# Recurrent attention and windowed attention in one kernel: the order of work between the two attentions, the places of VectorE's normalisations, and the banks at the head of a sequence

## The reference, cut to what matters

```
xn = layernorm(x)
# layer 0: gated recurrent attention, 16 heads of 16, times a mixture of 8 experts (top 2)
q, k, v = xn@Wq, xn@Wk, xn@Wv;  gate = exp(log_sigmoid(xn@Wgk1@Wgk2 + bgk2) / 16)
state = state * gate + outer(v, k);  out = state . q            # scan over the tokens
s = (layernorm(out) * gamma + beta) * silu(xn@Wg) @ Wout
f = sum over the top 2 experts e of gates[e] * (relu(xn@Wd[e] + bd[e]) @ Wu[e] + bu[e]) / 2
x = x + s * silu(f)
xn = layernorm(x)
# layer 1: attention in a window of 64 keys, 16 heads on 2 key heads, times a feed-forward net
s = softmax(q . k_window) . v_window @ Wo + bo
f = ternary(w_proj) applied to relu(ternary(w_fc) xn + gate * low-rank term)^2
x = x + s * silu(f)
```

## Time and profile before

| | |
|---|---|
| Time, median of 3 runs | 3416.82 us (3414.13 to 3417.32) |
| Profiled execution, its own time | 3419.85 us |
| Span of that execution (first to last instruction) | 3418.1 us |
| PE busy | 3286.0 us, 96% of the span |
| DVE, ACT, POOL busy | 2671.5 us (78%), 1834.8 us (54%), 1272.6 us (37%) |
| Chain that ended last, by engine | PE 71%, DVE 12%, ACT 7%, DMA 4%, issue 3%, POOL 1% |
| Granted TensorE clock, mean | 0.997 |

### The profile page before, as it was taken

The page is one execution under the profiler, slowest core; times in us unless marked ns, Lnnn a source line. Parts: engine busy times, 40 slices in busy tenths (PEclk is TensorE's granted clock), DMA queues, the critical chain, the costliest instruction groups (busy, mean ns, idle before and its releaser), DMA issues.

```text
span 3418.1 us, 89893 instructions
## 1 busy us (share of the span) xinstructions
PE 3286.0 (96%) x35134; PEld 2274.5 (67%) x35134; DVE 2671.5 (78%) x6395; ACT 1834.8 (54%) x4088; POOL 1272.6 (37%) x1404
## 2 busy tenths in 40 slices
PE   5999999999999999999999999999999999999998
PEld 3676666766667666676766667666676666766666
DVE  6877878878788777887778777787877878878787
ACT  3364654646546465463655636456364654646546
POOL 4434244242443524425233342423434244242432
PEclk9999999999999999999999999999999999999999
DMA  4002010020100202011020110202002010020110
GB/s 116 22 22 61 23 53 19 25 58 24 52 23 25 54 24 61 15 38 40 24 64 11 54 29 21 63 12 65 18 24 60 24 52 21 22 58 24 52 23 26
DMA packets 110005, 128.56 MB, mean 38 GB/s; under 512 B 23457, under 2 KB 77329, under 8 KB 109585
## 3 DMA queue, kind: packets, MB, share of 16 engines
q1 hardware_dynamic: 104720, 121.13, 13.7%
q10 hardware_dynamic: 4864, 1.69, 0.2%
HBM read 74.01 MB, written 17.30 MB: 27 GB/s over the span
## 4 chain that ended last, share of the span: by engine, by line
PE 71%; DVE 12%; ACT 7%; DMA 4%; issue 3%; POOL 1%; SPq 0%; DVEq 0%; ACTq 0%; POOLq 0%
PE bank L1926 7%; PE bank L1549 5%; PE bank L1945 5%; PE bank L1828 5%; PE bank L1694 4%; PE bank L1863 4%; PE bank L1889 4%; PE bank L1586 3%; DMA g_wide<-gate_rows 3%; PE bank L1711 3%; PE bank L1766 3%; PE bank L1666 3%; PE bank L1651 3%; DVE am L1268 3%; PE bank L1845 2%
## 5 line engine op out<-in xcount | busy, mean ns | idle before, releaser
L901 POOL TENSOR_TENSOR qx<-qx 128x512 f32<-128x512 f32 x256 | 277.5, 1084 | 656.9 <-ACT qx L1139 655.1
L1403 DVE TENSOR_REDUCE row_max<-bank 128x4 f32<-128x384 f32 x512 | 270.8, 550 | 90.6 <-PE bank L1828 90.1
L1268 DVE TENSOR_TENSOR am<-bank,causal 128x512 f32<-128x512 f32 x512 | 327.9, 682 | 17.6 <-PE bank L1666 17.6
L1509 DVE TENSOR_TENSOR sq_lo<-qx,sq_hi 128x512 fp32r<-128x512 f32 x256 | 232.3, 907 | 125.3 <-ACT sq_hi L1127 124.1
L1945 PE MATMUL bank<-pj_t,sq_hi 128*128 128x256 f32 x1024 | 260.3, 288 | 6.2 <-DVE sq_lo L1509 5.5
L1023 ACT ACTIVATE tanh_g<-bank 128x256 f32<-128x256 f32 x128 | 49.2, 384 | 400.8 <-PE bank L1549 400.8
L1549 PE MATMUL bank<-w_vg,xt 128*128 128x512 f32 x512 | 252.3, 615 | 0.0
L1945 PE MATMUL bank<-pj_t,sq_lo 128*128 128x256 f32 x1024 | 251.0, 279 | 0.0
L1586 PE MATMUL bank<-xt,w_down 128*128 128x512 f32 x512 | 237.2, 596 | 0.0
L1139 ACT ACTIVATE qx<-bank,scale_fc 128x512 f32<-128x512 f32 x256 | 177.2, 692 | 98.5 <-PE bank L1931 96.6
L1412 DVE TENSOR_TENSOR am<-bank,row_max 128x384 f32<-128x384 f32 x384 | 212.9, 554 | 9.8
(11 more groups left out here) (278 smaller groups left out, 8523.1 us busy)
## 6 DMA issues: line engine op xcount, KB each, us to landing
g_wide<-gate_rows SPq DMA_DIRECT2D x64, 512.0 KB, 6.1
x<-in_L_attn_x SPq DMA_DIRECT2D x128, 128.0 KB, 2.3
qt<-in_L_attn_x SPq DMA_DIRECT2D x128, 128.0 KB, 2.5
out<-x SPq DMA_DIRECT2D x128, 128.0 KB, 1.7
k<-k SPq DMA_DIRECT2D x96, 128.0 KB, 2.4
xl<-xh SPq DMA_DIRECT2D x48, 128.0 KB, 2.4
xl<-xn SPq DMA_DIRECT2D x48, 128.0 KB, 2.3
xh<-xn SPq DMA_DIRECT2D x48, 128.0 KB, 2.3
```

The lines of the kernel that those rows point to most:

```text
L901: nc.gpsimd.tensor_tensor(sq[:, n % 3, :], relu[:, n % 3, :], relu[:, n % 3, :], ALU.mult)\
L1268: nc.vector.tensor_tensor(am_tiles[:, :, j], bank[3 + j][:].rearrange("p (f e t) -> p f e t", f=2, e=2), causal[:].unsqueeze(1).unsqueeze( ...
L1403: nc.vector.tensor_reduce(row_max[:, j, :], bank[1 + j][:, 0:4 * KW].rearrange("p (h k) -> p h k", k=KW), AX.X, ALU.max, negate=(j == 0)). ...
L1509: nc.vector.tensor_tensor(sq_lo[:, n % 3, :], sq[:, n % 3, :], sq_hi[:, n % 3, :].bitcast(F32), ALU.subtract)\
```

## The change

It has three parts. (1) At the head of a sequence `experts_down(0)` to `(3)` and `first_queries_keys(6)` write to other banks, with other waits; ScalarE evicts the gate rows ahead of the queries 4 and 5. (2) On VectorE `finish_chunk(4)` moves from the end of chunk 5 into chunk 6, and two of the four `normalise2` of chunk 6 move behind `project_gated(5)`. (3) On PE `queries(0)` moves ahead of `output_project(7)`, to bank 2 instead of 5; `chunk_turn(7)` moves from behind `score_quad(0)` to the middle of `window_values(0)`.

```diff
+    down_banks = (2, 3, 7, 6)
+    first_banks = {2: 6, 3: 7, 4: 4, 5: 5, 6: 2, 7: 7}
-    qk_banks = (5, 1, 6, 0)
+    qk_banks = (2, 1, 6, 0)
 # ScalarE: first_queries_keys reads bank[first_banks[n]] instead of bank[4 + n % 4],
 # experts_relu reads bank[5 if g else down_banks[j]] instead of bank[5 if g else j]
                     experts_relu(0)
                     experts_relu(1)
-                    first_queries_keys(4)
-                    first_queries_keys(5)
                     for b in range(NG):
                         act.wait_ge(s["gtp_ok"], at("gtp_ok", b + 1))
                         nc.scalar.copy(gate_rows[:, b * 512:(b + 1) * 512], bank[gate_banks[b]][32:64, :]).then_inc(s["gx_ok"], 1)
+                    first_queries_keys(4)
+                    first_queries_keys(5)
                     experts_relu(2)
 # VectorE, chunk c
-                        if 2 <= c < NC - 2:
+                        if 2 <= c < NC - 1:
                             finish_chunk(c - 2)
                         if c == NC - 2:
                             dve.wait_ge(s["rs2"], at("rs2", 1))
-                            for b in range(4):
+                            for b in range(2):
                                 normalise2(b)
...
                             if c:
                                 project_gated(c - 1)
-                            if c == NC - 3:
-                                finish_chunk(c - 1)
+                            if c == NC - 2:
+                                for b in range(2, 4):
+                                    normalise2(b)
                             middle_state(c + 1)
 # PE, first_queries_keys
                         elif n >= 6:
-                            pe.wait_ge(s["qk_ok"], at("qk_ok", n - 5))
+                            pe.wait_ge(s["hr_ok"], at("hr_ok", 1 if n == 6 else 3))
 # PE, experts_down
-                        if i == 0:
-                            pass
-                            if copy:
-                                pe.wait_ge(s["lg_ok"], at("lg_ok"))
-                        elif i == 1:
-                            pass
-                            if copy:
-                                pe.wait_ge(s["hqk_ok"], at("hqk_ok"))
+                        if i in (2, 3):
+                            pe.wait_ge(s["qk_ok"], at("qk_ok", 4 - i))
 # PE, before the turns of the gates
                     pe.wait_ge(s["gates_ok"], at("gates_ok", 7))
-                    pe.wait_ge(s["hr_ok"], at("hr_ok", 2))
+                    if copy:
+                        pe.wait_ge(s["lg_ok"], at("lg_ok"))
 # PE, cumulate(0)
                             pe.wait_ge(s["qk_ok"], at("qk_ok", 3))
-                            pe.wait_ge(s["hr_ok"], at("hr_ok", 4))
+                            pe.wait_ge(s["hr_ok"], at("hr_ok", 2))
 # PE, parity_scores(0)
                             pe.wait_ge(s["qk_ok"], at("qk_ok", 5))
+                            pe.wait_ge(s["hr_ok"], at("hr_ok", 4))
 # PE, queries
-                        if n == 0:
-                            pe.wait_ge(s["f1_ok"], at("f1_ok", NC))
-                        elif n == 1:
+                        if n == 1:
                             pe.wait_ge(s["f2_ok"], at("f2_ok", NC - 1))
 # PE, window_values
                         for w in range(NC):
+                            if part == 0 and w == NC // 2:
+                                pe.wait_ge(s["sg_ok"], at("sg_ok", NC))
+                                chunk_turn(NC - 1)
 # PE, between the attentions
                     pair_turn(2)
                     queries(1)
                     output_turn(NC - 1)
+                    queries(0)
                     output_project(NC - 1)
-                    queries(0)
                     chunk_turn(6)
                     pe.wait_ge(s["low_ok"], at("low_ok", 1))
-                    pe.wait_ge(s["qk2_ok"], at("qk2_ok", 1))
+                    pe.wait_ge(s["qk2_ok"], at("qk2_ok", 2))
                     score_masks(0)
-                    pe.wait_ge(s["qk2_ok"], at("qk2_ok", 2))
                     score_quad(0)
-                    pe.wait_ge(s["sg_ok"], at("sg_ok", NC))
-                    chunk_turn(NC - 1)
                     window_values(0)
```

More of the change, by code:

```diff
@@ L917, in first_queries_keys @@
                         act.wait_ge(s["qkp_ok"], at("qkp_ok", n - 1))
-                        nc.scalar.copy((kt if which else qt)[:, half, g * 512:(g + 1) * 512], bank[4 + n % 4][:])\
+                        nc.scalar.copy((kt if which else qt)[:, half, g * 512:(g + 1) * 512], bank[first_banks[n]][:])\
                           .then_inc(s["qk_ok"], 1)
@@ L940, in experts_relu @@
                             act.wait_ge(s["gkl_ok"], at("gkl_ok", NC // 2))
-                        nc.scalar.activation(hidden_t[g][:, j, :], bank[5 if g else j][:], ACT.Relu, bias=b_down[:, j:j + 1])\
+                        nc.scalar.activation(hidden_t[g][:, j, :], bank[5 if g else down_banks[j]][:], ACT.Relu, bias=b_down[:, j:j + 1])\
                           .then_inc(s["hr_ok"], 1)
@@ L1566, in first_queries_keys @@
                         elif n >= 6:
-                            pe.wait_ge(s["qk_ok"], at("qk_ok", n - 5))
+                            pe.wait_ge(s["hr_ok"], at("hr_ok", 1 if n == 6 else 3))
                         w = w_k if which else w_q
                         for k in range(KD):
-                            mm = nc.tensor.matmul(bank[4 + n % 4][:], w[:, k, half * P:(half + 1) * P],
+                            mm = nc.tensor.matmul(bank[first_banks[n]][:], w[:, k, half * P:(half + 1) * P],
                                                   xt[:, k, g * 512:(g + 1) * 512], start=(k == 0), stop=(k == KD - 1))
@@ L1576, in experts_down @@
                         g, j = i // 4, i % 4
-                        if i == 0:
-                            pass
-                            if copy:
-                                pe.wait_ge(s["lg_ok"], at("lg_ok"))
-                        elif i == 1:
-                            pass
-                            if copy:
-                                pe.wait_ge(s["hqk_ok"], at("hqk_ok"))
+                        if i in (2, 3):
+                            pe.wait_ge(s["qk_ok"], at("qk_ok", 4 - i))
                         for k in range(KD):
-                            mm = nc.tensor.matmul(bank[5 if g else j][:], w_down[:, k, j * P:(j + 1) * P],
+                            mm = nc.tensor.matmul(bank[5 if g else down_banks[j]][:], w_down[:, k, j * P:(j + 1) * P],
                                                   xt[:, k, g * 512:(g + 1) * 512], start=(k == 0), stop=(k == KD - 1))
```

## The result

The changed kernel takes 3448.79 us (median of 4 runs, 3440.83 to 3453.05) against 3417.07 for the kernel before: ratio 1.0091, 95% interval 1.0074 to 1.0108, some +31 us. I had forecast 3425.4 us with a range to 3433, so the direction was right and the size was not.

A forecast was written before the change was run, and what follows sets the result against it. The prediction took TensorE (PE), busy 96% of the span, to bound the kernel, so only its waits counted. Terms -2.6 + 8.0 + 3.2 = +8.6 us on the median 3416.82 gave 3425.4 us, range 3411 to 3433.

The forecast's parts named there:

- the rest comes back as a longer wait at L1694: Sequence head, experts_up(0): PE's saved 1.38 us is kept only as far as GpSimd's product comes earlier; wait near 2.2 us.
- the -2.6 us that I took: Part 1's term: gate rows land 0.15 us earlier in 15 sequences and 0.4 in the first.
- the -0.4 that the rule cited from the Trainium skill's page gave: Part 1 if a DMA's semaphore write lands only after that engine's earlier writes: earlier issue behind the loads brings nothing.
- the gain at the issue: Sequence head: SP's write of the gate rows goes out 0.45 us earlier, right behind the loads of x.
- the lower of my two bounds: Part 1, sequence head: a gain of 0 us a sequence; the other bound was 0.45.
- the pull-in of 0.83 us: Chunk 6 on VectorE: its L1760 comes 5.64 us after its scores instead of 6.47.
- the sum into x at 1.17 us: Chunk 6 on VectorE: the moved sum runs beside GpSimd's product and was forecast to take 1.18 us.
- PE's wait before the second pair: Chunk 6: PE waits for normalised rows before pair_turn(1), so token_major(7) starts 0.5 us later, +8.0 us in all.
- The delay of queries(2): Between the attentions: output_project(7) ends 1.1 us later, so queries(2) starts 0.2 us later a sequence, +3.2 us in all.
- the product of GpSimd: Rival, sequence head: product in time, PE keeps its whole lead of 20.7 us; 3407.3 us, chance 0.08.
- the last turn of x: Rival, between the attentions: this turn is in time and part 3 gains 0.74 us a sequence; 3410.4 us, chance 0.07.
- a full gain at the head: Rival: gate rows land the full 0.45 us earlier, part 1 is -6.0, total 3422.0 us; 0.27 together with an unslowed sum into x.

The follow-up runs named there:

- e1: Part 1 alone on the kernel before: 3433.92 us, ratio 1.0038.
- e2: Part 1 on the kernel before, plus 16 extra identity turns per sequence ahead of experts_up(0) to keep PE busy in its wait: 3419.16 us, ratio 0.9998.
- e9: Part 1 on the kernel before, with the dropped wait for hr_ok 2 put back ahead of the gates' turns: 3416.14 us, ratio 0.9999.
- e6: Kernel before with only finish_chunk(4) moved into chunk 6, all four normalisations left in place: 3424.87 us, ratio 1.0017.
- e13: Part 3 on the kernel before, plus seven extra identity turns in PE's wait ahead of the last turn of x: 3420.64 us, ratio 1.0012.
- e8: Part 1 on the kernel before, with SP's eight loads of x issued behind the first broadcast of the gate rows: 3398.95 us, ratio 0.9940.
- e4: Part 3 alone on the kernel before: 3425.49 us, ratio 1.0025.
- e10: Kernel before with only SP's eight loads of x moved behind the first broadcast of the gate rows: 3409.92 us, ratio 0.9983.

## Why the prediction was right or wrong

**Part 1 (-2.6 us forecast, +16 measured): the step that failed.** It is the sentence "the rest comes back as a longer wait at L1694 (1.02 + 1.38 us less the gain)". The wait is as long as that (2.34 us on average), but I priced it at its own length, as if the matmuls behind it were the same. There was no term for the clock, neither in the sum nor among the bounds nor among the rivals. Behind a wait of that length they run at half the clock for 3 to 4 us, some 1.5 to 1.7 us lost each time, 12 times in the profiled execution of the change and 11 in that of e1. In e1's span, 19.1 us over the kernel before, PE's waits at the head are 4.2 us (38.6 against 34.4) and its busy time is 15.3 us. With the clock out of the way nothing is left of part 1's cost within some 3 us (e2: 0.9998, e9: 0.9999, with intervals of 0.001 to either side). These intervals can't tell the -2.6 us that I took from the -0.4 that the rule cited from the Trainium skill's page gave. The rows can: the gain at the issue (0.38 us) was lost at the landing (0.48), which is at the lower of my two bounds or just under it. The write-to-broadcast times (2.35, 1.87, 1.47) follow the loads in front; by that rule the trace agrees, though no run here tells it from a write that merely stands behind the loads' data in the queue.

I had the 1.00 of the granted clock in the kernel before in front of me at waits of 1.4 and 1.0 us and did not ask what their sum does. This case's trace shows the fall behind waits of 2.0 to 3.0 us, and behind one of 0.95 us that follows small tiles. The Trainium skill, TensorE: Matmul & The Clock Gate, section Part 1: The HAM clock gate, says that the slow level is the default and that recent activity keeps the fast one; the trace agrees, with 0.50 to 0.55 behind the merged wait.

**Part 2 (+8.0 forecast, +6.9 measured): right**, step by step: the pull-in of 0.83 us, the sum into x at 1.17 us beside GpSimd's product, PE's wait before the second pair. e6 puts the loss on the moved sum and statistics, as worked out.

**Part 3 (+3.2 forecast, +7.5 measured): mechanism right, one term too small and one missing.** The delay of queries(2) was 0.26 us a sequence, 4.2 us in all, where I had taken 0.2; e13 measures 4.7 with the clock held up. The missing term is the clock again, which likely makes up the rest.

**Sum.** Measured for the parts: 15.9 + 6.9 + 7.5 = 30.3 us, against about 31 for the whole. Each part is known to 3 to 5 us only, so that they agree so closely is partly luck. In hindsight, had I added 1.6 us for 12 falls at the head to the +8.6 and taken nothing for the gain of part 1, I had been at 3416.8 + 8.6 + 2.6 + 19.2 = 3447. The rivals on the fast side are out: the product of GpSimd was not in time, and the last turn of x was late. The one place where I had thought of a full gain at the head needs the loads of x out of SP's way (e8), which the change does not do.

## What to carry to other kernels

Before taking a wait away, look where the next one ends: if both are set by the same chain, they join, and a joined wait can cost more than the two did, because TensorE's clock often fell behind it here. Compare PE's busy time for the same number of matmuls before and after; when it rises, look at the granted clock window by window, not at its mean (0.997 to 0.990 went with some 19 us here). And when a chain goes through DMA, ask what stands in front of the write in the queue: here a write issued 0.38 us earlier behind the same loads let its reader start no earlier, while moving the loads gave 0.2% alone and 0.6% with the earlier copy.

## What was not expected of the hardware

- The clock fell to 0.50 for about 3.5 us behind PE waits of 2.0 to 3.0 us in 12 of 15 cases, but also behind waits of about 0.95 us in 5 of 16 (e4) where matmuls of 32 x 32 tiles stood in front; in the kernel before it never fell behind two waits of 1.4 and about 1 us that lay some 12 us apart. Nor did it behind three single waits of 2.1 to 2.3 us with the wait of 1.4 us still in front (e9, e10), where in e8, without it, it fell behind two of four waits over 2 us.
- 256 turns of the identity that compute nothing needed made a kernel 15 us faster (e2 against e1).
- A 16 KB write to DRAM took 1.47 us to the wake-up of its waiter with nothing in front, 1.87 when issued 0.4 us behind 1 MB of loads and 2.35 when issued directly behind them.
